# Moving a closing elementwise loop into the last matmul stage, and two weight prefetches behind the first down blocks

## What is computed

```python
xn = _layernorm(x, axis=-1)                      # x: 4 x 2048 x 4096
s = attention(xn, Wq, Wk, Wv, Wo)                # 32 heads, 8 kv heads, rope, causal
g = xn @ w_gate.T * s_gate                       # 4096 -> 11008
u = xn @ w_up.T * s_up
f = (silu(g) * u) @ w_down.T * s_down            # 11008 -> 4096
x = x + s * silu(f)
```

## Time and profile before

| What | us |
|---|---|
| median of three runs | 6506.57 |
| the profiled execution, its own time | 6505.81 |
| span of its slowest core (core 0) | 6504.3 |
| spans of all cores | 6457.9 to 6504.3 |
| TensorE busy (matmul) | 5568.6 |
| DMA: moved, mean rate | 543.88 MB, 84 GB/s |

### The profile page before, as it was taken

The page is one execution under the profiler, slowest core; times in us unless marked ns, Lnnn a source line. Parts: engine busy times, 40 slices in busy tenths (PEclk is TensorE's granted clock), DMA queues, the critical chain, the costliest instruction groups (busy, mean ns, idle before and its releaser), DMA issues.

```text
span 6504.3 us, 59675 instructions; the slowest of 8 cores (6457.9 to 6504.3 us)
## 1 busy us (share of the span) xinstructions
PE 5568.6 (86%) x25285; PEld 2524.5 (39%) x25792; DVE 976.3 (15%) x1206; ACT 778.0 (12%) x878; POOL 589.1 (9%) x400
## 2 busy tenths in 40 slices
PE   4676868787878999998889999789999799999981
PEld 2333333333333444444334444334444334444430
DVE  4444144444440000000000000000000000000004
ACT  1111022222221000000000000000000000000012
POOL 1111100000000111111000111000111000111000
PEclk7888889999999999999999999899999899999995
DMA  9999953333335887778545778653777654777437
GB/s 105 125 123 128 107 58 39 39 33 39 33 36 61 85 91 75 78 78 79 98 88 58 75 75 78 116 114 56 77 78 78 113 114 64 75 74 85 85 71 258
DMA packets 1414469, 543.88 MB, mean 84 GB/s; under 512 B 1275200, under 2 KB 1368000, under 8 KB 1414208
## 3 DMA queue, kind: packets, MB, share of 16 engines
q0 software_dynamic: 1327296, 421.55, 61.9%
q1 hardware_dynamic: 86912, 118.49, 6.0%
HBM read 902.80 MB, written 58.72 MB: 148 GB/s over the span
## 4 chain that ended last, share of the span: by engine, by line
PE 79%; DMA 8%; DVE 6%; ACT 4%; issue 3%; POOL 0%; DVEq 0%; SPq 0%; ACTq 0%; POOLq 0%
PE PS L801 19%; PE PS L691 18%; PE PS L700 18%; PE PS L445 7%; PE PS L627 4%; PE PS L320 3%; DMA WB<-wo 3%; PE PS L344 3%; PE PS L573 2%; DMA WB<-wv 2%; PE PS L578 2%; DVE R L593 2%; ACT R L546 2%; PE PS L536 1%; DMA R<-wdT 1%
## 5 line engine op out<-in xcount | busy, mean ns | idle before, releaser
L801 PE MATMUL PS<-R 128*128 128x512 bf16 x5395 | 1217.1, 386 | 114.1 <-DMA R<-wdT 78.1
L691 PE MATMUL PS<-R,WB 128*128 128x512 bf16 x5395 | 1202.0, 380 | 19.3 <-ACT R L824 12.2
L700 PE MATMUL PS<-R,WB 128*128 128x512 bf16 x5394 | 1195.7, 379 | 5.8
L801 PEld LDWEIGHTS PS<-R 128*128 128x128 bf16 x5504 | 546.5, 99 | 788.9 <-issue 164.1
L691 PEld LDWEIGHTS PS<-R,WB 128*128 128x128 bf16 x5504 | 539.6, 98 | 668.9 <-issue 24.2
L700 PEld LDWEIGHTS PS<-R,WB 128*128 128x128 bf16 x5504 | 538.7, 98 | 649.3
L734 DVE TENSOR_TENSOR R<-R 128x1024 bf16<-128x1024 bf16 x86 | 59.6, 693 | 3969.4 <-ACT R L725 3969.4
L627 PE MATMUL PS<-R,WB 128*128 128x512 bf16 x2007 | 450.5, 383 | 34.9 <-DMA WB<-wo 26.7
L445 PE MATMUL PS<-R,WB 128*128 128x512 bf16 x1942 | 432.9, 380 | 24.2 <-DVE R L464 22.1
L573 PE MATMUL PS<-R,ones_t 128*128 128x512 bf16 (+3 forms) x748 | 261.8, 364 | 213.5 <-DVE R L589 135.6
L546 ACT ACTIVATE R<-PS 128x1024 bf16<-128x1024 f32 (+3 forms) x384 | 304.3, 810 | 872.4 <-PE PS L536 872.4
(11 more groups left out here) (67 smaller groups left out, 2190.4 us busy)
## 6 DMA issues: line engine op xcount, KB each, us to landing
WB<-wuT POOLq DMA_DIRECT2D x86, 1024.0 KB, 15.4
WB<-wgT POOLq DMA_DIRECT2D x86, 1024.0 KB, 11.2
R<-wdT POOLq DMA_DIRECT2D x48, 1408.0 KB, 15.7
WB<-wk POOLq DMA_DIRECT2D x32, 1024.0 KB, 17.2
WB<-wv POOLq DMA_DIRECT2D x32, 1024.0 KB, 18.7
WB<-wo POOLq DMA_DIRECT2D x32, 1024.0 KB, 14.1
WB<-wq POOLq DMA_DIRECT2D x31, 1024.0 KB, 11.8
sp_hbm<-R SPq DMA_DIRECT2D x96, 256.0 KB, 7.6
```

The source lines that it names most:

```text
L691: fns.append(lambda eng, d=d, half=half, bsel=bsel, gbk=gbk: eng.matmul(PS[:, (gbk + half) * 512:(gbk + half + 1) * 512], wgb[bsel][:, d * ...
L700: fns.append(lambda eng, d=d, half=half, bsel=bsel, ubk=ubk: eng.matmul(PS[:, (ubk + half) * 512:(ubk + half + 1) * 512], wub[bsel][:, d * ...
L801: st=(qq == 0 and ii == 0), sp=(hf == 1 and ii == i1 - 1): eng.matmul(PS[:, (l * 2 + half) * 512:(l * 2 + half + 1) * 512], wdb[slot][:, i ...
```

## The change

Two things are moved, and one is split.

**Prefetches.** In the last two blocks of a gate/up stage the prefetch of the block after next is not issued but put on a list (`deferred_pf`). It is issued in the down stage, one after the second half of group 1 and one after that of group 2. In the last quarter there is nothing to fetch, and nothing on the list.

**Closing loop.** The loop at the end is gone. `f_chunk(hc)` does the work of one chunk and is called right after each eviction of the last quarter, so ScalarE's list has eviction and silu in turn. TensorE waits at the groups of that quarter (but the first) for the last eviction alone, not for the silu behind it. There are two buffers of each kind instead of four, at other places (`fxb2` in a free part of R2; `fgb2` where the gate/up stage's results stood). `f_loads(hc)` loads x and s for a chunk and is on GpSimd's list, no longer SyncE's; for chunks 0 and 1 it stands before group 0, for a later one it is called two chunks ahead and waits until the chunk that had the buffer has been added and its store has landed.

**Partial sums.** The load of `spv` for group hq + 1 now stands in SyncE's list right behind the injection of group hq, so ahead of the stores of group hq - 1's evictions.

```diff
+        def f_loads(hc):
+            b = hc % 2
+            if hc == 0:
+                wait("gpsimd", s_ss[0], s_ss[0].v)
+                wait("gpsimd", s_ss[1], s_ss[1].v)
+                for _q in range(4):
+                    wait("gpsimd", s_sp[_q], s_sp[_q].v)
+            elif hc >= 2:
+                wait("gpsimd", s_dv, v_fo_by[hc - 2])
+                wait("gpsimd", s_o[b], v_out_by[hc - 2])
+            dma("gpsimd", fxb2[b], x_ownT[hc * 128:(hc + 1) * 128, :], s_f[b])
+            v_fs_by[hc] = dma("gpsimd", fsb2[b], sT_hbm[hc * 128:(hc + 1) * 128, :], s_f[b])
+
+        def f_chunk(hc):
+            b = hc % 2
...
+            elif hc >= 2:
+                wait("scalar", s_dv, v_fo_by[hc - 2])
+            wait("scalar", s_ac, a_ev_last_box[0])
+            a_si = op("scalar", lambda eng, hc=hc, b=b: eng.activation(
+                fgb2[b], s_ffnT[:, hc * 1024:(hc + 1) * 1024], AF.Silu), s_ac)
+            wait("vector", s_ac, a_si)
+            wait("vector", s_f[b], v_fs_by[hc])
+            v_fo_by[hc] = chain("vector", [
+                lambda eng, b=b: eng.tensor_mul(fgb2[b], fsb2[b], fgb2[b]),
+                lambda eng, b=b: eng.tensor_add(fxb2[b], fxb2[b], fgb2[b])], s_dv)
+            wait("sync", s_dv, v_fo_by[hc])
+            v_out_by[hc] = dma("sync", out_T[hc * 128:(hc + 1) * 128, :], fxb2[b], s_o[b])
+            if hc + 2 < DC:
+                f_loads(hc + 2)
...
                 if i + 2 < IC:
-                    wait("gpsimd", s_pe, v_u)
-                    prefetch_gu(i + 2, i % 2)
+                    if ii >= sz - 2:
+                        deferred_pf.append((i + 2, i % 2, v_u))
+                    else:
+                        wait("gpsimd", s_pe, v_u)
+                        prefetch_gu(i + 2, i % 2)
...
+            if qq == 3:
+                f_loads(0)
+                f_loads(1)
...
-                wait("tensor", s_ac, s_ac.v)
+                if qq == 3 and hq >= 1:
+                    wait("tensor", s_ac, a_ev_last_box[0])
+                else:
+                    wait("tensor", s_ac, s_ac.v)
...
                     v_inj_prev = group("tensor", fns, s_pe)
+                    if hq + 1 < 8:
+                        wait("sync", s_pe, v_inj_prev)
+                        vsp_by[hq + 1] = spv_loads(hq + 1)
...
+                if deferred_pf and hq in (1, 2):
+                    pi, pb, pvu = deferred_pf.pop(0)
+                    wait("gpsimd", s_pe, pvu)
+                    prefetch_gu(pi, pb)
...
+                        a_ev_last_box[0] = op("scalar", lambda eng, l=l, hc=hc: eng.activation(
...
+                        f_chunk(hc)
```

More of the change, by code:

```diff
@@ L187, in build_nc @@
         us_b = R3[:, 17408:19456]
-        fxb = [R3f[:, i * 1024:(i + 1) * 1024] for i in range(4)]
-        fsb4 = [R3[:, 8192 + i * 1024:8192 + (i + 1) * 1024] for i in range(4)]
-        fgb4 = [R3f[:, 6144 + i * 1024:6144 + (i + 1) * 1024] for i in range(4)]
+        R2f = R2.bitcast(F32)
+        fxb2 = [R2f[:, 14080 + i * 1024:14080 + (i + 1) * 1024] for i in range(2)]
+        fsb2 = [R3[:, 19456 + i * 1024:19456 + (i + 1) * 1024] for i in range(2)]
+        fgb2 = [R3f[:, 7680 + i * 1024:7680 + (i + 1) * 1024] for i in range(2)]
         def bank(i):
@@ L671, in build_nc @@
         v_spdma_by = {}
+        v_fo_by = {}
+        v_out_by = {}
+        v_fs_by = {}
+        a_ev_last_box = [0]
+        deferred_pf = []
+        def f_loads(hc):
[12 more added lines that the diff above has]
+            b = hc % 2
+            if hc == 0:
+                wait("scalar", s_dv, v_hT[IC - 1])
+                for _q in range(4):
+                    wait("scalar", s_sp[_q], s_sp[_q].v)
+            elif hc >= 2:
[12 more added lines that the diff above has]
+                f_loads(hc + 2)
         for qq in range(4):
@@ L762, in build_nc, with spv_loads @@
             wd_dma(1)
-            for hq in range(8):
-                vsp = [0] * 4
-                if qq > 0:
-                    if hq == 0:
-                        for _q in range(4):
-                            wait("sync", s_sp[_q], s_sp[_q].v)
-                    if v_inj_prev is not None:
-                        wait("sync", s_pe, v_inj_prev)
-                    for l in range(4):
-                        hc = hq * 4 + l
-                        vsp[l] = dma("sync", spv[:, l * 1024:(l + 1) * 1024],
-                                     sp_hbm[1 - par, hc * 128:(hc + 1) * 128, :], s_spv)
+            def spv_loads(hq):
+                return [dma("sync", spv[:, l * 1024:(l + 1) * 1024],
+                            sp_hbm[1 - par, (hq * 4 + l) * 128:(hq * 4 + l + 1) * 128, :], s_spv)
+                        for l in range(4)]
+            vsp_by = {}
+            if qq > 0:
+                for _q in range(4):
+                    wait("sync", s_sp[_q], s_sp[_q].v)
+                if v_inj_prev is not None:
+                    wait("sync", s_pe, v_inj_prev)
+                vsp_by[0] = spv_loads(0)
+            if qq == 3:
+                f_loads(0)
+                f_loads(1)
+            for hq in range(8):
                 if hq == 0:
                     wait("tensor", s_dv, v_hT[base + sz - 1])
-                wait("tensor", s_ac, s_ac.v)
+                if qq == 3 and hq >= 1:
+                    wait("tensor", s_ac, a_ev_last_box[0])
+                else:
+                    wait("tensor", s_ac, s_ac.v)
                 if qq > 0:
-                    wait("tensor", s_spv, vsp[3])
+                    wait("tensor", s_spv, vsp_by[hq][3])
                     fns = []
@@ L845, in build_nc @@
             dma("sync", sffn_dbg, s_ffnT[:], s_dbg)
-        wait("sync", s_ac, a_ffn_done)
-        v_fo_by = {}
-        v_out_by = {}
-        for hc in range(DC + 2):
-            if hc < DC:
-                b = hc % 4
-                if hc >= 4:
-                    wait("sync", s_dv, v_fo_by[hc - 4])
-                    wait("sync", s_o[b], v_out_by[hc - 4])
-                dma("sync", fxb[b][:], x_ownT[hc * 128:(hc + 1) * 128, :], s_f[b])
-                vs = dma("sync", fsb4[b][:], sT_hbm[hc * 128:(hc + 1) * 128, :], s_f[b])
-                if hc == 0:
-                    wait("scalar", s_ac, a_ffn_done)
-                if hc >= 4:
-                    wait("scalar", s_dv, v_fo_by[hc - 4])
-                a_si = op("scalar", lambda eng, hc=hc, b=b: eng.activation(
-                    fgb4[b][:], s_ffnT[:, hc * 1024:(hc + 1) * 1024], AF.Silu), s_ac)
-                wait("vector", s_ac, a_si)
-                wait("vector", s_f[b], vs)
-                v_o = chain("vector", [
-                    lambda eng, b=b: eng.tensor_mul(fgb4[b][:], fsb4[b][:], fgb4[b][:]),
-                    lambda eng, b=b: eng.tensor_add(fxb[b][:], fxb[b][:], fgb4[b][:])], s_dv)
-                v_fo_by[hc] = v_o
-            sc = hc - 2
-            if 0 <= sc < DC:
-                sb = sc % 4
-                wait("sync", s_dv, v_fo_by[sc])
-                v_out_by[sc] = dma("sync", out_T[sc * 128:(sc + 1) * 128, :], fxb[sb][:], s_o[sb])
         for _sm in (s_cst, s_ck, s_kst, s_vst, s_kk[0], s_kk[1], s_kvv, s_spv,
```

1 line of the change is left out of this document (removed).

## The result

Against the kernel before, the changed kernel takes 0.9724 of the time, 95% interval 0.9689 to 0.9758: 2.8% less, which on 6506.57 us is 6327 us, 180 us saved. In six of the nine timed runs one die or both ran at a lower granted clock and took 6868 us or more, and six of the ten of the kernel before were longer in the same way (6637 us and more), so the ratio is of the others (6316.83, 6328.76 and 6343.28 us), while the median over all nine, the time on record, is 7177.3 us and outside the range of the forecast.

A forecast was written before the change was run, and what follows sets the result against it. TensorE was taken to bound the kernel up to 6361.87 us, the closing loop from there. Terms -79.6 - 117.9 + 24.0 + 3.5 = -170.0 us took the median 6506.57 to 6336 us, range 6320 to 6376.

The forecast's parts named there:

- The three waits for a block: Start of the first three quarters' down stages: issuing down blocks ahead of two prefetches saves 79.6 us.
- The step that set each quarter against the last one: Quarter starts: priced each stall against the last quarter, which has none; gains 24.5, 27.6 and 27.5 us.
- The closing loop: End of the kernel: moving silu, multiply, add and store into the last down stage cuts 142.4 to 24.5 us, gaining 117.9.
- The working to 24.5: After the last matmul: eviction, silu, add, store, reload of two buffers and final store add up to 24.5 us.
- The chain on GpSimd's queue: Last quarter: down blocks queue behind chunk loads awaiting stores, issued some 34 us after a group's end, ten us to spare.
- The boundaries: Seven group boundaries of the last down stage: silus between evictions lengthen TensorE's wait from 4.5 to 7.9 us, costing 24.0.
- The extra for the clock: Same seven boundaries: the longer wait keeps TensorE's clock low longer, 0.5 us each, 3.5 us in all.
- The first block isn't early: Rival, quarter starts: something besides queue place holds the block, so 79.6 us are not gained; 6416 us, chance 0.07.
- Late blocks: Rival, last quarter: landings doubled make down blocks 12.6 us late for six groups, 76 us; 6412 us, chance 0.12.
- Slower than before: Rival, last quarter: landings four times as long make blocks 73 us late for six groups; 6773 us, chance 0.03.
- The shared SBUF interface: Last down stage: VectorE's two-input multiplies and adds might hold GpSimd's issues; no cost counted, at worst about 2.5 us at the end.
- from the sum to the time: Whole kernel: took 170.0 us off the profiled 6505.81 us and the median 6506.57, giving 6335.8 and 6336.6 us.

The follow-up runs named there:

- the single buffer: Changed kernel with evictions ahead of the silus and one x and s buffer instead of two; lowest run 6418.42 us against 6521.35 for the kernel before.
- the last run: Changed kernel with evictions first, own buffers for chunks 30 and 31, and TensorE waiting for each chunk's eviction alone; ratio 0.9582 to the kernel before.

## Why the prediction was right, and where it was wrong

The forecast of 170 us less stands against 176.1 on core 0 and a ratio that says 180, with an interval of about 22 us to each side; the forecast of a time, 6336 us with a range of 6320 to 6376, stands against a median of 7177.3. Term by term:

- **The three waits for a block.** Forecast 79.6, measured 82.2 alone. Most of the difference is in the first quarter, where the prediction counted the wait and left out the lower clock behind it, which it counted in the other two: on core 0 the first eviction came 26.85 us and 3139.83 - 3099.61 = 40.22 us behind the last up matmul before, and 2.37 us and 3107.15 - 3068.91 = 38.24 us behind it with the prefetches moved, together 26.5 us less and not 24.5. The step that set each quarter against the last one held: from its injection to its first eviction the second quarter was to take 41.7 us and takes 4100.50 - 4058.90 = 41.6 (timeline of the changed kernel, core 1, against the earlier trace rows):

```profile
4058.90 3.46 PE L835 MATMUL PS<-R,iden_t 128*128 128x512 bf16 x8 [2.37 <-DVE R L778]
...
4100.50 3.77 ACT L883 ACTIVATE R<-PS 128x1024 bf16<-128x1024 f32 x4 [42.75 <-PE PS L856]
```

- **The closing loop.** Forecast 117.9, measured 142.4 - 22.1 = 120.3 on core 0, and 118.2 as the mean of the eight cores (138.7 to 142.5 us before, 22.2 to 23.0 after). The working to 24.5 was 1.6 us too long against the 22.9 of core 1: a store lands in 2.7 us (median) when it isn't one of many, I took 4.6, and the least of the earlier trace rows, 2.6, would have been right; the loads were 0.8 us quicker too, and the first adds 0.6 us later than worked out. The chain on GpSimd's queue was too long for the same reason, since there I took 6.6 us for a store, twice in a row: the block is issued 26 us behind a group's end, not 34. The stores of the down stage in the changed kernel, core 1, against the earlier trace rows:

```profile
DMA to landing us min/median/max: 2.6/2.7/5.2
```

- **The boundaries.** Forecast 24.0 for the silus, measured 47.80 - 44.32 = 3.48 us at seven (mean periods over the last quarter, core 1 of the changed kernel and core 0 of the one before), 24.3. The extra for the clock, 3.5, is not there: in the changed kernel the injection runs at the lower level just as before the change, and the clock is up again as soon behind it (first window an injection, second what follows; core 1):

```profile
6093.00:6096.30 3.30, 3.30 (x9) 1.07 (x9) 0.00 (x0) 1.02 (x1) 1.11 (x2) 0.50 0.56 179
6096.30:6098.00 1.70, 1.70 (x9) 0.83 (x8) 0.00 (x0) 0.00 (x0) 1.06 (x2) 0.95 0.84 260
```

- **The rivals.** "The first block isn't early" fell with the waits gone. "Late blocks" did not come, but the single buffer shows that it was the right thing to fear, and that its price was worked out wrongly: 12.6 us late for six groups is not 76 us, since a block is ordered two groups ahead and the delay is shared by both periods. "Slower than before" did not come.
- **The shared SBUF interface.** The Trainium skill (GPSIMD Engine Reference, Specifications) speaks of contention with VectorE instructions that have two SBUF inputs. In the last down stage and behind it GpSimd's issues hardly ever ran beside one: on core 1 of the changed kernel none did, on core 0 three loads did (at 6219.30, 6219.82 and 6266.69), and they took 0.53, 0.54 and 0.53 us, as those with VectorE idle. So no cost is seen, but the two engines met too seldom to test it.

The step that failed is the last one, from the sum to the time: "So 6335.8, and 6336.6 by the median". I took the median of three runs, 6506.57, as the time of the kernel, although one of the three was 6873.96, and gave the range no room for that. The ten runs of the kernel before that stand beside the result have a median of 6658.86, and six of the nine of the changed one are above 6860, so a range up to 6376 fails against their median of 7177.3. No term of the sum is in that: the three mechanisms held, and each size within 4 us. The lower end of the range was thin as well: the bounds named (-7 us) give 6329, the text says 6320 without working it out, and the shortest run took 6316.83. Why single runs of one kernel lie this far apart, and whether the change has a part in it, was not tested and stays open.

## What to carry to other kernels

A prefetch that waits for the last product of a stage holds back everything behind it on its queue, so put what the next stage needs first ahead of it. A closing loop can hide inside the last matmul stage, but what is put between two evictions is paid by TensorE at every boundary: evict first, then do the rest, and let TensorE wait for the bank that it writes, not for the group. Each shortening of the period takes room from the queue that feeds it, so look at that queue again after each. To price such a change, set the stage against one in the same profile that already has the form wanted (here the last quarter), take landing times of lone transfers for lone transfers, and where three runs differ by 6%, let the forecast of a time have room for the longest of them, or forecast the difference alone.

## What was not expected of the hardware

- A wait of 7.9 us costs TensorE no more clock than one of 4.5 us: in both cases the injection behind it runs at the lower level (0.50 and 0.53) and the clock is back within some 4 us. Held back in four steps of 0.4 to 1.4 us instead, TensorE kept a granted clock of 1.00 through the injection at six boundaries of seven (last quarter, core 0 of the last run), and the down matmuls behind it come at once at 0.219 us each.
- A store of 512 KB takes 2.7 us to land (median, changed kernel) among other traffic at a DMA share of 0.65, where the same store in the old closing loop took 6.6 at a share of 0.89. That fits queueing by the loop's own transfers; no run tests it apart.
